# The keep mask of a graph dilation: removals and their transposes summed in PSUM, and the mask written by ScalarE instead of VectorE

## The chip, the cores and the metric

One Trainium2 chip, one of its cores. The metric is the device time of the whole program in microseconds, median over runs. The core has a matrix engine (TensorE, PE in the rows; PEld is its weight load), VectorE (DVE), ScalarE (ACT), GpSimd (POOL) and a queue for transfers (SyncE, SP). Matmuls write into PSUM, which DVE and ACT can read.

## The reference

16 graphs of 1024 nodes with 128 features; `adj` is 16 x 1024 x 1024. Two layers. The first makes three rounds of

```
h = h @ W + b
cos = normalized(h) @ normalized(h).T
h = (adj * cos) @ h            # relu but for the last
```

The second first thins the graph out. Row after row, every `sf`-th neighbour is removed, and each removal also takes the mirrored entry out of the later rows:

```
def step(carry, n):
    row = carry[n]; num = sum(row)
    sf = where(num > 10, (num + 1) // 2, 1)
    rm = row & (cumsum(row) % sf == 0)   # only where mask and num > 1
    carry = carry.at[n].set(row & ~rm)
    carry = carry.at[:, n].set(carry[:, n] & ~rm)
```

It multiplies `adj` by what is left and makes three graph convolutions with batch norms on it. With the inputs given `adj` is symmetric in its pattern, but not in its values.

## The kernel before

The program has a large first part, `layer0`, from 0 to about 1865 us, and then the stages of the second layer. In `layer0` two kinds of work run side by side on the same engines.

The one is the first layer: 48 units (a graph and a round), each of 16 half steps. For a half step PE makes one 128x512 block of the cosine from three fp32r matmuls (L529 to L531), DVE multiplies it by `adj` (L717), and PE aggregates (L538, an fp32 matmul that shows as two rows). The cosine is made two half steps ahead; there are two PSUM tiles for it and three for the product. At fixed half steps of a unit come the short steps of its ends: `ha` the 16 rows of the next projection (L510), `hb` the bias sum on DVE (L695) and then the eight squares with a row sum on ACT (L611), `hc` and `hd` the rest of the row norm, `hf` transposes on PE and a copy on ACT (L622), `evac` the copy of a finished aggregation (L626), and for a new graph `lna` (statistics on DVE, a sqrt on ACT), `lnb` (scaling on DVE, L685), `lnc` (transposes, then relu on ACT) and `posta`/`postb` (transposes, residual sum on DVE).

The other is the thinning, whose result is the mask of entries to keep, stored in DRAM as bytes. It goes in four quads of four graphs. For each of eight blocks of 128 rows a fixpoint of ranks and removals is found (`rule`, `drop`, `again`, L488, L640, L776), then the whole row block is ranked (`wide`: L575 on PE, L650 on ACT, L795 on DVE writes the removals `R`, fp8). After the eight blocks of a quad come its 32 `mask` steps, m = 0 to 127 in all. One makes the mask of 128 rows by 1024 columns in two halves of 512 (j). PE transposes four 128x128 blocks of `R` by a matmul with the identity into half j of the PSUM tile `Dp` (L590). DVE compares: it keeps 1 where the transposed removal is below 0.5 and that is greater than the row's own removal, and writes it into `kp` (L805), one of two tiles. SP stores the tile. PE's matmuls for half j of mask m wait until half j of mask m-1 has been read (semaphore `kp`), and the writing of mask m waits for the store of mask m-2 (semaphores `kps0` and `kps1`).

One plan, made by `layer0_plan` before the program is built, fixes the order on every engine: each engine goes through the same list and does its own part of each step, in that order. Steps of the thinning are spread over the half steps by a weight each; a mask has weight 1, and about one mask step falls to a half step (the 32 of a quad over 34 or 35 half steps). In the mask stretches `hb` occurs at seven places: units 12 and 13, 24 and 25, 35 and 36, and 47. For units 12, 24, 25, 36 and 47 a mask stands in the same half step behind `hb` and another in the next half step; for 13 and 35 the first mask behind `hb` comes in the half step after it.

There is a second writer of masks, `dilate_all`, that runs only where the fixpoint has not settled; it is not touched.

Of the kernel before, what the change touches and what calls it, by code (L numbers as in the profile page):

```python
# [13 lines left out]
ALU = mybir.AluOpType  # L14
ACT = mybir.ActivationFunctionType
# [5 lines left out]
NK = 8  # L21
# [20 lines left out]
def half(j):  # L42
    return slice(j * 512, j * 512 + 512)
# [322 lines left out]
def layer0(nc, A, C, S):  # L366
    with ExitStack() as ctx:
# [3 lines left out]
        T = P.sems("ats0 ats1 at af0 af1 af2 sign low au x ct ru vr sd v8 wd av b1 rw tr kp kps0 kps1")  # L371
# [17 lines left out]
        R = [P.sb(f"R{i}", [128, NK, N], FP8) for i in range(Q)]  # L389
# [12 lines left out]
        kp = [P.sb(f"kp{i}", [128, N], FP8) for i in range(2)]  # L402
        sm = {n: P.sb(f"sm_{n}", [128, Q]) for n in ("t", "sf", "sc", "va", "h", "b", "c", "b2")}
        Dp = P.ps("D", [128, 2, 512])
# [76 lines left out]
        def pe(e):  # L481
            def transposes(src, done):
                for k in range(NK):
                    t = e.transpose(pp[:, k, :], src(k), C["ident"][:])
                t.then_inc(done, 1)

            def count(i, src):
                e.matmul(rank(i)[:, 0:129], src, C["U2"][:, 0:129], start=True, stop=True).then_inc(T["ct"], 1)  # L488

            for kind, *a in plan:  # L490
                if kind == "lnc":
                    g, = a
                    e.wait_ge(E["lnr"], g + 1)
                    if g == 1:
                        e.wait_ge(E["nl"], 1)
                    elif g > 1:
                        e.wait_ge(E["xadd"], g - 1)
                    transposes(lambda k: tmp[:, k, :], E["tln"])
                elif kind == "ha":
                    u, = a  # L500
                    g, i = UNITS[u]
                    if u == 0:
                        e.wait_ge(E["w"], 32)
                    if i == 0:
                        e.wait_ge(E["relu"], g + 1)
                    else:
                        e.wait_ge(E["ev"], 2 * (u - 2) + 2)
                        e.wait_ge(E["nl"], u)
                    for k in range(NK):
                        t = e.matmul(pp[:, k, :], hT[g % 2][:, blk(k)], W[:, i, :], start=True, stop=True)  # L510
                    t.then_inc(E["ph"], 1)
                elif kind == "hf":
                    u, = a
                    e.wait_ge(E["vn"], u + 1)
                    transposes(lambda k: tmp[:, k, :], E["tnh"])
                elif kind == "posta":
                    u, = a
                    e.wait_ge(E["ev"], 2 * u + 2)
                    e.wait_ge(E["nl"], min(u + 2, 3 * G))
                    transposes(lambda k: hT[UNITS[u][0] % 2][:, blk(k)], E["tpost"])  # L520
                elif kind == "cos":
                    idx, = a
                    u, k, j = idx // 16, idx % 16 // 2, idx % 2
                    n, m = nh[u % 2], nl[u % 2]
                    if idx % 16 == 0:
                        e.wait_ge(E["nl"], u + 1)
                    if idx > 1:
                        e.wait_ge(E["ew"], idx - 1)
                    e.matmul(cos[j][:], n[:, blk(k)], n[:, half(j)], start=True, stop=False)  # L529
                    e.matmul(cos[j][:], n[:, blk(k)], m[:, half(j)], start=False, stop=False)  # L530
                    e.matmul(cos[j][:], m[:, blk(k)], n[:, half(j)], start=False, stop=True).then_inc(E["cos"], 1)  # L531
                elif kind == "agg":
                    idx, = a
                    u, k, j = idx // 16, idx % 16 // 2, idx % 2
                    e.wait_ge(E["ew"], idx + 1)
                    if k == 0 and u:
                        e.wait_ge(E["ev"], 2 * (u - 1) + j + 1)
                    e.matmul(acc[j][:], Hr[u % 2][:, k, :], ew[idx % 3][:], start=(k == 0),  # L538
                             stop=(k == NK - 1)).then_inc(E["agg"], 1)
                elif kind == "first":  # L540
                    n, i = a
                    quad, k = divmod(n, NK)
                    if k:
                        e.wait_ge(T["low"], lows(n, i))
                    else:
                        e.wait_ge(T["at"], 64 * quad + 8 * k + 2 * i + 2)
                        if quad and i == 0:
                            e.wait_ge(T["kp"], 64 * quad)
                    others = [q for q in range(NK) if q != k]
                    for q in others:  # L550
                        e.matmul(rank(i)[:, 132:134], AT[i][:, q, blk(k)], (C["two1"] if q < k else C["zero1"])[:],
                                 start=(q == others[0]), stop=(q == others[-1]))
                    count(i, AT[i][:, k, blk(k)])
                elif kind == "again":
                    n, r = a
                    rr = round_of(n, r)
                    for i in range(Q):
                        if i % 2 == 0:
                            e.wait_ge(T["vr"], Q * rr + i + 2)
                        e.wait_ge(T["sd"], Q * rr + i + 1)  # L560
                        count(i, Sd[i][(r + 1) % 2][:])
                elif kind == "wide":
                    n, i, j = a
                    k, K = n % NK, ROUNDS[n % NK]
                    rr = round_of(n, K - 1)
                    if i == 0:
                        e.wait_ge(T["vr"], Q * rr + (2 if j == 0 else 4))
                    elif j == 0:
                        e.wait_ge(T["b1"], Q * n + i)
                    else:  # L570
                        e.wait_ge(T["av"], 8 * n + 2 * i)
                    if j == 0:
                        e.wait_ge(T["sd"], Q * rr + i + 1)
                    for q in range(4 * j, 4 * j + 4):
                        t = e.matmul(Dp[:, j, q * 128 - j * 512:512],  # L575
                                     Sd[i][K % 2][:] if q == k else AT[i][:, q, blk(k)],
                                     C["UL"][:, 0:512 - (q * 128 - j * 512)], start=(q == 4 * j),
                                     stop=(q == 4 * j + 3), skip_group_check=True)
                    t.then_inc(T["wd"], 1)
                elif kind == "mask":  # L580
                    m, = a
                    quad, i, q = m // 32, m % 32 // NK, m % NK
                    for j in range(2):
                        if m % 32 == 0:
                            e.wait_ge(T["rw"], 64 * (quad + 1))
                            e.wait_ge(T["b1"], Q * NK * (quad + 1))
                        else:
                            e.wait_ge(T["kp"], 2 * (m - 1) + j + 1)
                        for b in range(4):
                            t = e.matmul(Dp[:, j, blk(b)], R[i][:, 4 * j + b, blk(q)], C["ident8"][:],  # L590
                                         start=True, stop=True)
                        t.then_inc(T["tr"], 1)

        def act(e):
            for kind, *a in plan:
# [27 lines left out]
                elif kind == "evac":  # L623
                    u, j = a
# [17 lines left out]
                elif kind == "wide":  # L642
                    n, i, j = a
# [9 lines left out]
                    if j == 0:  # L653
                        if n:
                            e.wait_ge(T["av"], 8 * (n - 1) + 2 * i + 2)
                        e.activation(b1[:, i:i + 1], Dp[:, 0, 511:512], ACT.Identity, bias=sm["b"][:, i:i + 1],
                                     scale=sm["sc"][:, i:i + 1]).then_inc(T["b1"], 1)

        def dve(e):
            Dv = Dp[:, :, 0:288].rearrange("p b (i c) -> p b i c", c=144)  # L660
# [2 lines left out]
            for kind, *a in plan:  # L663
# [125 lines left out]
                elif kind == "row_out":  # L789
# [3 lines left out]
                    if quad and k == 0:  # L793
# [1 line left out]
                    e.scalar_tensor_tensor(R[i][:, k, half(j)], v[c % 3][:], sm["sf"][:, i:i + 1],  # L795
                                           Ab[Q * (n % 2) + i][:, half(j)], ALU.not_equal, ALU.is_lt,
                                           saturate=False).then_inc(T["rw"], 1)
                elif kind == "mask":
                    m, = a
                    quad, i, q = m // 32, m % 32 // NK, m % NK  # L800
                    if m > 1:
                        e.wait_ge(T[f"kps{m % 2}"], 16 * (m // 2))
                    for j in range(2):
                        e.wait_ge(T["tr"], 2 * m + j + 1)
                        e.scalar_tensor_tensor(kp[m % 2][:, half(j)], Dp[:, j, :], 0.5, R[i][:, q, half(j)],  # L805
                                               ALU.is_lt, ALU.is_gt, saturate=False).then_inc(T["kp"], 1)

        run(nc, pe, act, dve, pool, sp)

# [901 lines left out]
```

## Time and profile before

| | us |
|---|---|
| median of 3 runs | 3062.6 (3059.87 to 3064.27) |
| the profiled execution | 3064.47 |
| its span in the profile | 3062.4 |
| busy, share of the span: PE | 90% |
| DVE | 77% |
| ACT | 41% |
| POOL | 37% |

Busy is the time in which an engine had at least one instruction in flight. Matmuls overlap one another, so that a matmul's own duration is longer than what it takes of PE; the distance between starts tells the latter. In the order of time, rows of equal instructions in sequence are merged, and "xN" is their number. The bracket behind a row is idle time before it and who ended it.

### The profile page before, as it was taken

How to read it: one execution, taken by the hardware profiler on the slowest of the kernel's cores; microseconds unless marked ns; L12 is line 12 of the kernel's file. 1: busy time of each engine (PE TensorE's matmuls, PEld its weight loads, DVE VectorE, ACT ScalarE, POOL GpSimd, SP SyncE). 2: the span in 40 equal slices, each digit the busy share in tenths (PEclk: the TensorE clock that was granted, in tenths of full speed). 3: DMA queues.
4: the chain of work that ended last, by engine and by line, in shares of the span. 5: the costliest groups of instructions: out<-in, count | busy, mean ns of one | idle time of the engine just before them, and what ended most of it. 6: DMA issues, size and time to landing. Idle time of an engine off the chain costs nothing. (4 is left out here: it accounts for less than half of the span.)

```text
span 3062.4 us, 40924 instructions
## 1 busy us (share of the span) xinstructions
PE 2763.8 (90%) x13317; PEld 1741.2 (57%) x13366; DVE 2352.1 (77%) x6136; ACT 1269.0 (41%) x3748; POOL 1126.7 (37%) x509
## 2 busy tenths in 40 slices
PE   6988999998999998899998995999999979998776
PEld 4655656655656655566655563555555545555666
DVE  4888998898988898888888885756566436775887
ACT  2545541554531555432545420223332234443664
POOL 4434333433432333330000002766666404444772
PEclk9999999999999999999999997999999989998888
DMA  6455346446336336326124014255544229994442
GB/s 217 126 159 179 107 125 198 129 138 198 108 98 209 121 111 207 92 86 201 62 81 154 18 42 171 104 204 218 196 186 184 105 103 394 397 397 171 153 165 117
DMA packets 304077, 492.26 MB, mean 161 GB/s; under 512 B 18544, under 2 KB 196080, under 8 KB 303856
## 3 DMA queue, kind: packets, MB, share of 16 engines
q1 hardware_dynamic: 303856, 489.57, 46.1%
q8 instruction: 108, 1.77, 0.2%
q14 instruction: 113, 0.93, 0.1%
HBM read 422.38 MB, written 67.11 MB: 160 GB/s over the span
## 5 line engine op out<-in xcount | busy, mean ns | idle before, releaser
L478 POOL TENSOR_SCALAR a_AT<-a_ats 128x512 uint8<-128x512 f32 x256 | 503.2, 1970 | 872.3 <-DMA a_ats<-in_adjT 820.4
L538 PE MATMUL a_acc<-a_ew,a_Hr 128*128 128x512 f32 x1536 | 794.0, 599 | 2.6 <-ACT a_hT L626 2.5
L717 DVE TENSOR_TENSOR a_ew<-adj,a_cos 128x512 f32<-128x512 f32 x768 | 522.7, 682 | 141.4 <-PE a_cos L531 140.2
L529 PE MATMUL a_cos<-a_nh 128*128 128x512 f32 x768 | 445.9, 581 | 2.4 <-DVE a_nl L709 2.4
L1286 POOL TENSOR_TENSOR b_dsum<-adj 128x1024 f32<-128x1024 f32 x16 | 141.9, 8868 | 661.1 <-DVE adj L1240 661.1
L538 PEld LDWEIGHTS a_acc<-a_ew,a_Hr 128*128 128x128 f32 x1536 | 291.9, 190 | 72.8 <-issue 2.2
L640 ACT ACTIVATE a_vr<-a_D,a_sm_b,a_sm_sc 128x128 f16<-128x128 f32 x560 | 210.0, 455 | 248.2 <-DVE a_sm_b L766 247.5
L531 PE MATMUL a_cos<-a_nh,a_nl 128*128 128x512 f32 x768 | 306.0, 398 | 0.0
L530 PE MATMUL a_cos<-a_nl,a_nh 128*128 128x512 f32 x768 | 305.9, 398 | 0.0
L1130 PE MATMUL b_acc<-adj,b_h 128*128 128x512 f32 x512 | 224.9, 597 | 23.4 <-DVE adj L1240 23.4
L1290 POOL TENSOR_TENSOR b_dsum<-b_dsum,adj 128x1024 f32<-128x1024 f32 x96 | 225.7, 2351 | 14.1 <-POOL b_dsum L1290 0.5
L1130 PE MATMUL b_acc<-adj,b_z 128*128 128x512 f32 x512 | 223.6, 595 | 0.0
L1387 PE MATMUL c_acc<-adj,c_z 128*128 128x512 f32 x512 | 222.4, 592 | 0.0
L776 DVE SCALAR_TENSOR_TENSOR a_Sd<-a_vr,a_sm_sf,a_X 128x128 fp8e4<-128x128 f16 x560 | 193.9, 371 | 12.1 <-ACT a_vr L640 11.3
L795 DVE SCALAR_TENSOR_TENSOR a_R<-a_v,a_sm_sf,a_Ab 128x512 fp8e4<-128x512 f16 x256 | 186.7, 768 | 9.9 <-ACT a_v L650 9.8
L805 DVE SCALAR_TENSOR_TENSOR a_kp<-a_D,a_R 128x512 fp8e4<-128x512 f32 x256 | 164.6, 685 | 36.9 <-PE a_D L590 30.6
L1477 POOL TENSOR_TENSOR adj<-adj,c_kp 128x1024 f32<-128x1024 f32 x52 | 102.9, 2010 | 242.3 <-DMA adj<-in_adjT 242.3
L611 ACT ACTIVATE a_tmp<-a_Hr 128x128 f32<-128x128 f32 x384 | 113.1, 295 | 187.1 <-DVE a_Hr L695 187.1
L529 PEld LDWEIGHTS a_cos<-a_nh 128*128 128x128 f32 x768 | 147.9, 193 | 63.7 <-issue 55.9
L530 PEld LDWEIGHTS a_cos<-a_nl,a_nh 128*128 128x128 f32 x768 | 148.4, 193 | 57.2 <-issue 56.7
L1130 PEld LDWEIGHTS b_acc<-adj,b_h 128*128 128x128 f32 x512 | 96.9, 192 | 139.7 <-issue 114.2
L531 PEld LDWEIGHTS a_cos<-a_nh,a_nl 128*128 128x128 f32 x768 | 146.1, 190 | 33.7
(198 smaller groups left out, 4875.4 us busy)
## 6 DMA issues: line engine op xcount, KB each, us to landing
adj<-in_adjT SPq DMA_DIRECT2D x108, 1024.0 KB, 12.7
adj<-in_adjT SPq DMA_DIRECT2D x128, 512.0 KB, 5.7
a_ats<-in_adjT SPq DMA_DIRECT2D x256, 256.0 KB, 3.4
a_af<-in_adj SPq DMA_DIRECT2D x256, 256.0 KB, 3.4
scr_keep<-a_kp SPq DMA_DIRECT2D x128, 128.0 KB, 1.8
b_kp<-scr_keep SPq DMA_DIRECT2D x16, 1024.0 KB, 8.4
c_zi<-scr_z SPq DMA_DIRECT2D x32, 512.0 KB, 5.4
c_ai<-scr_ag SPq DMA_DIRECT2D x32, 512.0 KB, 6.4
```

The lines of the kernel that those rows point to most:

```text
L478: e.tensor_scalar(AT[i][:, 4 * h:4 * h + 4, blk(k)].bitcast(U8), ats[h][:], 0.0, ONE8, ALU.is_gt, ALU.mult).then_inc(T["at"], 1)
L529: e.matmul(cos[j][:], n[:, blk(k)], n[:, half(j)], start=True, stop=False)
L530: e.matmul(cos[j][:], n[:, blk(k)], m[:, half(j)], start=False, stop=False)
L531: e.matmul(cos[j][:], m[:, blk(k)], n[:, half(j)], start=False, stop=True).then_inc(E["cos"], 1)
L538: e.matmul(acc[j][:], Hr[u % 2][:, k, :], ew[idx % 3][:], start=(k == 0), stop=(k == NK - 1)).then_inc(E["agg"], 1)
L640: e.activation(vr[:, i, :], rank(i)[:, 0:128], ACT.Abs, bias=sm["b2"][:, i:i + 1], scale=sm["sc"][:, i:i + 1]).then_inc(T["vr"], 1)
L717: e.tensor_tensor(ew[idx % 3][:], adj[g % 2][:, k, half(j)], cos[j][:], ALU.mult).then_inc(E["ew"], 1)
L776: e.scalar_tensor_tensor(Sd[i][(r + 1) % 2][:], vr[:, i, :], sm["sf"][:, i:i + 1], X[i][:], ALU.is_equal, ALU.is_lt, saturate=False).then_ ...
L795: e.scalar_tensor_tensor(R[i][:, k, half(j)], v[c % 3][:], sm["sf"][:, i:i + 1], Ab[Q * (n % 2) + i][:, half(j)], ALU.not_equal, ALU.is_lt ...
L1130: t = e.matmul(acc[j][:], src[:, q, :], adj[n % 3][:, q, half(j)], start=(q == 0), stop=(q == NK - 1))
L1290: e.tensor_tensor(d[:], d[:], b[:, q, :], ALU.add).then_inc(E["ds"], 1)
L1387: t = e.matmul(acc[j][:], z[m % 2][:, q, :], adj[slot(m)][:, q, half(j)], start=(q == 0), stop=(q == NK - 1))
```

## The change

The transposes of the removals are now added to the removals themselves in PSUM: one more matmul for each half, with the identity as weights and the row's own 512 columns of `R` as the moving operand, is issued first and starts the accumulation; the four transposing ones add to it. The sum is 0, 1 or 2. The mask is then relu(1 - sum), written by ACT from that PSUM half into the same fp8 tile. The step `mask` is taken out of DVE's list and put into ACT's at the same place of the plan, with the same waits.

```diff
                         else:
                             e.wait_ge(T["kp"], 2 * (m - 1) + j + 1)
+                        e.matmul(Dp[:, j, :], C["ident8"][:], R[i][:, q, half(j)], start=True, stop=False,
+                                 skip_group_check=True)
                         for b in range(4):
                             t = e.matmul(Dp[:, j, blk(b)], R[i][:, 4 * j + b, blk(q)], C["ident8"][:],
-                                         start=True, stop=True)
+                                         start=False, stop=True, skip_group_check=True)
                         t.then_inc(T["tr"], 1)
```

In `act`:

```diff
+                elif kind == "mask":
+                    m, = a
+                    if m > 1:
+                        e.wait_ge(T[f"kps{m % 2}"], 16 * (m // 2))
+                    for j in range(2):
+                        e.wait_ge(T["tr"], 2 * m + j + 1)
+                        e.activation(kp[m % 2][:, half(j)], Dp[:, j, :], ACT.Relu, bias=1.0, scale=-1.0,
+                                     saturate=False).then_inc(T["kp"], 1)
```

In `dve`:

```diff
-                elif kind == "mask":
-                    m, = a
-                    quad, i, q = m // 32, m % 32 // NK, m % NK
-                    if m > 1:
-                        e.wait_ge(T[f"kps{m % 2}"], 16 * (m // 2))
-                    for j in range(2):
-                        e.wait_ge(T["tr"], 2 * m + j + 1)
-                        e.scalar_tensor_tensor(kp[m % 2][:, half(j)], Dp[:, j, :], 0.5, R[i][:, q, half(j)],
-                                               ALU.is_lt, ALU.is_gt, saturate=False).then_inc(T["kp"], 1)
```

## Rows read from the trace of the kernel before

**Rows 1.** The page, first part: busy us, share of the span, instructions.
```profile
PE 2763.8 (90%) x13317; PEld 1741.2 (57%) x13366; DVE 2352.1 (77%) x6136; ACT 1269.0 (41%) x3748; POOL 1126.7 (37%) x509
```

**Rows 2.** Busy us of each engine in the four mask stretches, granted clock, DMA.
```profile
core 0: us, PE busy (x) PEld busy (x) DVE busy (x) ACT busy (x) POOL busy (x), PEclk, DMA share, GB/s
439.80:530.70 90.90, 83.67 (x504) 55.41 (x504) 77.96 (x159) 13.60 (x46) 27.79 (x15) 0.96 0.64 203
890.00:980.00 90.00, 82.28 (x494) 53.82 (x493) 77.68 (x160) 12.61 (x45) 25.06 (x13) 0.98 0.66 209
1340.00:1430.00 90.00, 83.61 (x504) 55.25 (x502) 79.48 (x163) 12.90 (x46) 11.53 (x6) 0.98 0.51 162
1786.80:1862.20 75.40, 74.22 (x457) 48.20 (x457) 65.67 (x105) 6.70 (x24) 0.00 (x0) 1.00 0.22 76
```

**Rows 3.** Groups by line: busy us, mean ns | idle just before, who ended it.
```profile
L590 PE MATMUL a_D<-ident,a_R 128*128 128x128 fp8e4 x1024 | 84.9, 221 | 23.8 <-DVE a_kp L805 22.0 <-DVE a_R L795 0.8
...
L805 DVE SCALAR_TENSOR_TENSOR a_kp<-a_D,a_R 128x512 fp8e4<-128x512 f32 x256 | 164.6, 685 | 36.9 <-PE a_D L590 30.6
```

**Rows 4.** Order of time (start, us) in the first stretch: layer norm, mask, PE's wait.
```profile
450.15 2.14 DVE L685 TENSOR_SCALAR a_tmp<-a_tmp,a_lnmv,a_lnrs 128x128 f32<-128x128 f32 x8
...
452.20 1.29 DVE L805 SCALAR_TENSOR_TENSOR a_kp<-a_D,a_R 128x512 fp8e4<-128x512 f32 x2
...
452.95 0.40 PE L590 MATMUL a_D<-ident,a_R 128*128 128x128 fp8e4 x4 [2.18 <-DVE a_kp L805]
```

**Rows 5.** PE in order of time, fourth stretch: a step without a mask, one with.
```profile
1792.21 1.02 PE L538 MATMUL a_acc<-a_ew,a_Hr 128*128 128x512 f32 x2
...
1793.77 1.02 PE L538 MATMUL a_acc<-a_ew,a_Hr 128*128 128x512 f32 x2
...
1795.82 1.02 PE L538 MATMUL a_acc<-a_ew,a_Hr 128*128 128x512 f32 x2
1796.68 0.61 PE L590 MATMUL a_D<-ident,a_R 128*128 128x128 fp8e4 x8
...
1797.41 0.40 PE L530 MATMUL a_cos<-a_nl,a_nh 128*128 128x512 f32 x1
1797.64 0.40 PE L531 MATMUL a_cos<-a_nh,a_nl 128*128 128x512 f32 x1
1797.88 1.02 PE L538 MATMUL a_acc<-a_ew,a_Hr 128*128 128x512 f32 x2
```

**Rows 6.** PE's groups by shape: matmuls with fp8 weights, 512 and 128 columns.
```profile
L575 PE MATMUL a_D<-UL,a_AT 128*128 128x512 bf16 x180 | 68.8, 382 | 8.7 <-ACT a_b L656 7.3 <-ACT a_v L650 1.4
...
L575 PE MATMUL a_D<-UL,a_AT 128*128 128x128 bf16 x224 | 49.1, 219 | 0.0
```

**Rows 7.** ACT's groups by shape, to 1865 us.
```profile
L634 ACT ACTIVATE a_Ab<-a_af 128x512 fp8e4<-128x512 f32 x256 | 153.6, 630 | 26.4 <-DMA a_af<-in_adj 26.2
L611 ACT ACTIVATE a_tmp<-a_Hr 128x128 f32<-128x128 f32 x384 | 113.1, 295 | 187.1 <-DVE a_Hr L695 187.1
L650 ACT ACTIVATE a_v<-a_D,a_b,a_sm_sc 128x512 f16<-128x512 f32 x128 | 99.5, 777 | 17.9 <-DVE a_R L795 3.7 <-PE a_D L575 0.8
...
L626 ACT ACTIVATE a_hT<-a_acc 128x512 f32<-128x512 f32 x96 | 57.6, 600 | 153.6 <-PE a_acc L538 153.5
L622 ACT ACTIVATE a_nh<-a_pp 128x1024 fp32r<-128x1024 f32 x48 | 49.4, 1028 | 135.8 <-PE a_pp L484 135.8
```

**Rows 8.** Order of time in the fourth stretch, around the one `hb`.
```profile
1805.84 1.02 PE L538 MATMUL a_acc<-a_ew,a_Hr 128*128 128x512 f32 x2
...
1806.34 0.68 DVE L717 TENSOR_TENSOR a_ew<-adj,a_cos 128x512 f32<-128x512 f32 x1
...
1806.93 1.22 DVE L695 TENSOR_TENSOR a_Hr<-a_pp,a_rows 128x1024 f32<-128x1024 f32 x1
```

**Rows 9.** Who waited for whom: us in total, times, longest us.
```profile
DVE a_kp L805 <- DMA scr_keep<-a_kp: 6.1, 6, 1.4
```

## The prediction

> **What bounds the kernel now.** I read the page's first part, then the four stretches in which the keep masks are made, then who waits for whom in them, and last the order of time in single steps. TensorE (PE) is busy for 90% of the span, VectorE (DVE) for 77% and ScalarE (ACT) for 41% [rows 1]. By these shares the change moves work from the second busiest engine to an idle one, and adds some to the busiest. What that is worth is read only where the masks are made, in four stretches of about 32 masks each, 346.3 us together [rows 2]. There ACT is nearly idle (12.6 to 13.6 us of 90, and 6.7 of 75.4), while PE and DVE both run near full: 83.67 and 77.96 of 90.90 in the first, 74.22 and 65.67 of 75.40 in the fourth. So the two share the limit. In the fourth PE is it, with 1.2 us left over. In the first three PE lacks 7.2, 7.7 and 6.4 us (length less busy), and its clock, which is granted at one of two levels (2.4 and 1.2 GHz), has means of 0.96, 0.98 and 0.98 of the higher.
>
> The same idle time by its cause: over all 1024 transposing matmuls PE stood 22.0 us waiting for DVE's mask (L805) [rows 3]. Where it comes from is seen at 450 us: DVE has the residual sum and the layer-norm scaling to do (L685, 2.14 us), writes the mask after it (452.20), and PE, which needs the mask tile's PSUM half read, idles 2.18 us [rows 4]. Between such places PE has no gap. From one aggregation (L538) to the next it takes 1793.77-1792.21 = 1.56 us without a mask step and 1797.88-1795.82 = 2.06 us with one [rows 5], so the eight 128-column matmuls of a mask cost PE 0.50 us, 62 ns each. The 221 ns of their row [rows 3] is their length from start to end, much of it overlapped, and no price. DVE in such a step does two masks of 0.685 us and one product L717 of 0.68 us, 2.05 us of work beside PE's 2.06.
>
> **What is removed from DVE.** 256 instructions at 685 ns (counted in halves of a mask), 175 us [rows 3] (the page's 164.6 us counts overlapped starts once). Of it only what PE now waits for can come back: the 22.0 us of waits, and the clock that fell behind them. Over the first three stretches that is 90.9 x 0.04 + 90 x 0.02 + 90 x 0.02 = 7.2 us [rows 2]. With DVE at 0.68 us per step against PE's 2 us and more, even the 3.6 us that it spends at a time on the residual sum and layer norm is made good before the next product is due. I take back all of it: -29.2 us. Outside the four stretches no mask is made and nothing changes.
>
> **What is added to PE.** One pass of 512 fp8 columns for each half, 256 in all. No such row exists. From below: a wide matmul of L575 with fp8 weights takes 219 ns at 128 columns and 382 at 512 [rows 6], 163 ns for 384 more columns, so 0.217 us for 512. From above: the 512-column fp32r passes of the cosine start 1797.64-1797.41 = 0.23 us and 1797.88-1797.64 = 0.24 us apart, weights loaded under the one before [rows 5]. I take 0.22: 256 x 0.22 = 56.3 us (0.217 gives 55.6, 0.235 gives 60.2). The furthest bound below is the 62 ns of one small mask matmul, 16 us. The added weight load is counted in the spacing, as those of L530 and L531 are. None of it is hidden: PE has no gap left once the masks come in time. Accumulating instead of overwriting is taken at nothing, since the cosine's three passes accumulate at that same spacing.
>
> The Trainium skill ("TensorE: Matmul & The Clock Gate", Back-to-back issue gap) puts a sustained stream of weight load and matmul at about 131 ns for 512 columns, and the isolated gap at N/2.4 + 2.5 ns, 216 ns. The trace contradicts the first (0.23 us in a stream with loads, rows 5) and supports the second. By 131 ns the pass would cost an estimated 33.5 us in place of 56.3, and the forecast would be 23 us lower.
>
> **What is added to ACT.** 256 instructions, 128x512 fp8 out of PSUM. The nearest rows: 600 ns for the copy L626 from PSUM with constants, 630 for the fp8 sign L634, 777 for L650 with both scale and bias from memory [rows 7]. So an operand from memory adds about 90 ns. If the constant bias of one is read as a column, 0.69 us is the value, and I take it; the ends are 0.60 and 0.78. Sum 177 us of work, in steps that now last 2.06 + 0.44 = 2.5 us, where a mask takes ACT 1.38 us. It fits, and costs nothing by itself.
>
> But ACT works in the order of the plan, and PE's next mask half waits for the one before to be read. What ACT has queued ahead of a mask now counts. Evacuations (0.60 us) and copies of 1024 columns (1.03 us) end before PE has done its mask, cosine and aggregation (2.5 us). The sqrt of the layer norm waits for 2.3 us of statistics on DVE; counted from the end of the cosine it is ready near 3.6 us, its mask half at 4.2, and PE comes for it at 4.4 after an aggregation, a mask, another product and the transposes. That just fits. The squares of the row norm (`hb`) do not. They wait for DVE's bias sum L695, which waits its turn behind L717. After the cosine's end (PE's aggregation starts at 1805.84 [rows 8]): product from 0.2 to 0.88 us, bias sum of 1.22 to 2.1 (1806.93 to 1808.15 now, because the masks are ahead of it), ACT's squares 8 x 0.295 = 2.36 us [rows 7] to 4.55, mask halves at 5.2 and 5.9. PE arrives for the first at 0.86 + 0.94 + 1.56 = 3.4 us. It waits 1.9 us and some 0.2 more for the second half: 2.1 us. In the plan `hb` falls into the mask stretches seven times; five times with a mask in its own step and in the next, 5 x 2.1 = 10.5 us, twice with the masks one step later, 2 x 0.4 = 0.8. Sum 11.3 us. Waits of this length are of the size after which the clock fell before (2.18 us at 452.95, clock 0.96 in that stretch). I take two falls at 1.8 us each, what the second and the third stretch lost with 0.98: +3.6 us.
>
> **Moved with it.** The wait for the store of the mask two before moves from DVE to ACT: 6.1 us in 6 waits, the longest 1.4 [rows 9]. SP's order is the same, its store is issued when the mask is written, and PE sees the wait only through ACT; behind it on ACT stand the same masks as before. Nothing more.
>
> **The sum.** -22.0 - 7.2 + 56.3 + 11.3 + 3.6 = +42.0 us. The profiled execution took 3064.47 us (span 3062.4), 1.9 above the median of 3062.6, so on the median 3104.6, in round numbers 3105.
>
> **The rivals.**
> R1, ACT holds PE more often. The sqrt of the layer norm just fits; if the mask takes 0.78 us or the handshakes are slower, its seven places and others give waits of 1 to 2 us, another 11 us, with 4 us of clock and the pass at 0.235: +42.0 + 11 + 4 + 3.9 = +60.9, about 3124. For it: three engines in turn. Against it: ACT's 1.1 us of slack in each step.
> R2, the squares do not hold PE. If the product and the bias sum come early enough, or the semaphores allow a step of run-ahead that I missed, the 14.9 us go: +27.1, 3090. Against it: the two PSUM halves are the only ones.
> R3, the other side: faster. The new pass costs PE no more than the small matmuls around it, 62 ns, since the price is that of issuing one and not of its columns. Then 256 x 0.0625 = 16.0 us against 29.2 back, and with ACT never late it is -13.2: 3049. It decides below 29.2/256 = 0.114 us per pass. Against it stands the 163 ns between 128 and 512 columns [rows 6].
> R4, PE is not full. PE's weight loads are busy for 48.20 of 75.40 us in the fullest stretch [rows 2]; if matmul busy overstates it, part of the new passes lies in room that the rows don't show. Half of them hidden: +13.6, 3076. Against it: the unbroken spacing of rows 5, where no start is free. The Trainium skill ("Perfetto Trace Analysis", Identifying the Most-Contended Engine) says that matmul occupancy is no good measure and weight-load busy is; by it the 64% here means headroom, against which the start-to-start times speak.
>
> **How the numbers follow.** Forecast (+33 to +52) 0.62; R1 0.15; R2 0.12; R4 and a cheap pass 0.06, of which 0.03 end within 0.2%; R3 0.05. The change is certain to do its work on ACT instead of DVE; no case for that. Within 0.2% means 6 us, about what a measurement of this kernel can tell from none. Faster 0.05, same 0.03, slower 0.92. The range leaves out R3, R4 and the far end of R1: 3086 to 3125.
>
> **What would show it.** The fourth stretch near 91 us in place of 75.4 (32 x 0.44 = 14 us for the passes, 2 us for its one `hb`, less a little waiting); the first three 94 to 101 us each, the passes being partly paid by what PE waited. PE's step with a mask 2.50 us. DVE's busy share down by 165 us, ACT's up by 150 to 180. PE's waits for a mask on ACT near 11 us, in places of about 2 us after L611. The fourth stretch under 83 us would make the price of the pass wrong; the first three shorter than before would bring R3; waits for ACT over 20 us, R1.

## The result, and the profile after

The changed kernel takes 3086.23 us (median of 4 runs, 3085.45 to 3088.13) against 3061.23 us (3059.15 to 3064.27): ratio 1.0085, 95% interval 1.0072 to 1.0097. Run again beside the experiments it gave 3084.93 us and 1.0080 (1.0066 to 1.0094). It is slower by 25 us. I had forecast slower by 42, 3105 us, with a range of 3086 to 3125: the side is right and the size is off by 17 us. The value lies 0.2 us above the lower end of the range, and the second measurement 1 us below it.

The first part of the page after (busy us, share, instructions):

```profile
PE 2809.2 (91%) x13622; PEld 1767.0 (57%) x13622; DVE 2194.5 (71%) x5880; ACT 1403.9 (46%) x4004; POOL 1126.9 (37%) x509
```

Against [rows 1] DVE has lost 157.6 us of work and ACT gained 134.9, and PE has gained 45.4 us. DVE's work did not set the time: PE's busy time grew by 45.4 us, its idle time shrank by 24.1, and the span grew by the difference, 21.3 us (3083.7 - 3062.4). The masks' lines, by shape (busy us, mean ns | idle before, who ended it):

```profile
L589 PE MATMUL a_D<-a_R,ident 128*128 128x512 fp8e4 x256 | 97.1, 379 | 8.5 <-ACT a_kp L666 7.7 <-DVE a_R L805 0.8
...
L592 PE MATMUL a_D<-ident,a_R 128*128 128x128 fp8e4 x1024 | 98.9, 219 | 0.0
```

PE waits for the mask 7.7 us where it waited 22.0 [rows 3]. The four stretches, each now cut from the start of its first mask matmul to the start of its last one (length, busy us by engine, granted clock):

```profile
440.50:533.80 93.30, 91.77 (x570) 60.33 (x569) 41.90 (x97) 46.04 (x109) 28.88 (x15) 1.00 0.61 199
890.50:985.40 94.90, 91.82 (x572) 60.32 (x571) 43.79 (x99) 45.22 (x107) 25.00 (x13) 1.00 0.64 202
1344.20:1437.50 93.30, 91.76 (x572) 60.42 (x570) 41.91 (x97) 44.60 (x106) 11.53 (x6) 1.00 0.51 160
1794.20:1881.30 87.10, 85.52 (x518) 54.35 (x519) 28.10 (x40) 39.88 (x86) 0.00 (x0) 1.00 0.19 64
```

Cut in the same way, the stretches of the kernel before are:

```profile
440.00:530.80 90.80, 83.57 (x506) 55.37 (x505) 77.86 (x159) 13.60 (x46) 27.89 (x15) 0.96 0.64 203
892.50:983.30 90.80, 82.51 (x507) 54.27 (x505) 78.44 (x160) 12.40 (x44) 25.06 (x13) 0.98 0.66 209
1343.20:1431.20 88.00, 81.61 (x506) 54.54 (x505) 77.44 (x159) 11.53 (x44) 11.53 (x6) 0.98 0.53 169
1786.90:1861.00 74.10, 73.07 (x454) 47.88 (x455) 64.44 (x103) 6.53 (x23) 0.00 (x0) 1.00 0.22 75
```

The sums are 368.6 and 343.7 us: 24.9 us arise here, where the spans differ by 21.3, so the rest of the program is 3.6 us shorter. I take that remainder for scatter: no instruction in the rest was changed, and over the ten profiled executions of this document it took between 2709 and 2719 us. In the fourth stretch, where PE waited least before, the change costs most: 13.0 us, against 2.5, 4.1 and 5.3 in the others.

In single steps, PE in the fourth stretch (start, us):

```profile
1809.87 1.02 PE L538 MATMUL a_acc<-a_ew,a_Hr 128*128 128x512 f32 x2
1810.73 0.38 PE L589 MATMUL a_D<-a_R,ident 128*128 128x512 fp8e4 x1
1810.95 0.39 PE L592 MATMUL a_D<-ident,a_R 128*128 128x128 fp8e4 x4
1811.17 0.38 PE L589 MATMUL a_D<-a_R,ident 128*128 128x512 fp8e4 x1
1811.38 0.39 PE L592 MATMUL a_D<-ident,a_R 128*128 128x128 fp8e4 x4
...
1812.35 1.02 PE L538 MATMUL a_acc<-a_ew,a_Hr 128*128 128x512 f32 x2
```

From aggregation to aggregation it takes 2.48 us in place of 2.06 [rows 5]. That is 0.42 us for two passes, 0.21 each, and 128 x 0.42 = 53.8 us in all.

And the place behind the squares, the one in the fourth stretch, first PE and then ACT:

```profile
1816.62 1.02 PE L538 MATMUL a_acc<-a_ew,a_Hr 128*128 128x512 f32 x2
...
1819.10 1.02 PE L538 MATMUL a_acc<-a_ew,a_Hr 128*128 128x512 f32 x2
1821.65 0.39 PE L589 MATMUL a_D<-a_R,ident 128*128 128x512 fp8e4 x1 [1.54 <-ACT a_kp L666]
...
1823.34 1.02 PE L538 MATMUL a_acc<-a_ew,a_Hr 128*128 128x512 f32 x2
```

```profile
1818.67 0.31 ACT L613 ACTIVATE a_tmp<-a_Hr 128x128 f32<-128x128 f32 x1 [1.90 <-DVE a_Hr L705]
...
1821.03 1.05 ACT L666 ACTIVATE a_kp<-a_D 128x512 fp8e4<-128x512 f32 x2
```

ACT gets the bias sum, makes the squares from 1818.67 on, and writes the waiting mask only at 1821.03. PE's step from 1819.10 to 1823.34 is 4.24 us instead of 2.48, so 1.76 us are lost. The plan has five such places in the mask stretches, and the trace has exactly five waits of PE for ACT's mask.

### The profile page after: what moved, and what is told of

Read it like the earlier page. It is cut to its first block and busy times, and to the rows that moved or that the text cites. A ratio compares the mean times of both kernels' runs of the same rounds, so it can differ in the third digit from the quotient of the medians.

```text
span 3083.7 us, 41485 instructions
## 1 busy us (share of the span) xinstructions
PE 2809.2 (91%) x13622; PEld 1767.0 (57%) x13622; DVE 2194.5 (71%) x5880; ACT 1403.9 (46%) x4004; POOL 1126.9 (37%) x509
## 5 line engine op out<-in xcount | busy, mean ns | idle before, releaser
L786 DVE SCALAR_TENSOR_TENSOR a_Sd<-a_vr,a_sm_sf,a_X 128x128 fp8e4<-128x128 f16 x560 | 191.4, 369 | 12.7 <-ACT a_vr L642 11.7
L666 ACT ACTIVATE a_kp<-a_D 128x512 fp8e4<-128x512 f32 x256 | 138.6, 593 | 120.6 <-PE a_D L592 114.1
L575 PE MATMUL a_D<-UL,a_AT 128*128 128x384 bf16 (+3 forms) x896 | 156.4, 299 | 13.7 <-ACT a_b L658 7.3
```

The source lines that it names most:

```text
L786: e.scalar_tensor_tensor(Sd[i][(r + 1) % 2][:], vr[:, i, :], sm["sf"][:, i:i + 1], X[i][:], ALU.is_equal, ALU.is_lt, saturate=False).then_ ...
```

## The experiments

All ratios are to the kernel before on the same chip (3062.10 us for e1 to e4, 3060.88 for e5 to e7 and the changed kernel run again; the first two lines of the table are the first pair). "Stretches" is the sum of the four lengths, cut as above. "Waits" is PE's idle time before a mask matmul by the trace, in us. "Floor" is what PE needs in the stretches without a wait: 359.5 us with the passes (shown under `e4_mask_before_squares`), 359.5 - 53.8 = 305.7 us without.

| kernel | us | ratio (95%) | stretches | PE's waits for a mask |
|---|---|---|---|---|
| before | 3061.23 | | 343.7 | 22.0 |
| changed | 3086.23 | 1.0085 (1.0072 to 1.0097) | 368.6 | 7.7 |
| e1_no_pass | 3042.21 | 0.9929 (0.9907 to 0.9951) | 323.6 | 10.3 |
| e2_pass_on_dve | 3088.79 | 1.0083 (1.0062 to 1.0104) | 372.2 | 10.5 |
| e3_two_passes | 3137.92 | 1.0240 (1.0216 to 1.0263) | 421.2 | 5.5 |
| e4_mask_before_squares | 3077.69 | 1.0043 (1.0027 to 1.0060) | 359.5 | 0 |
| e5_split_ln | 3044.17 | 0.9949 (0.9935 to 0.9962) | 328.0 | 8.6 |
| e6_split_wide | 3044.62 | 0.9950 (0.9936 to 0.9963) | 325.4 | 0.2 |
| e7_split_narrow | 3044.15 | 0.9951 (0.9935 to 0.9966) | 325.8 | 7.9 |

**e1_no_pass**: ScalarE writes the mask, without the added matmul.

```diff
-                        e.matmul(Dp[:, j, :], C["ident8"][:], R[i][:, q, half(j)], start=True, stop=False,
-                                 skip_group_check=True)
...
-                                         start=False, stop=True, skip_group_check=True)
+                                         start=True, stop=True)
```

> The changed kernel without the added pass: the four transposing matmuls overwrite as before, and ScalarE writes relu(1 - transposes). It leaves out the row's own removals from the mask. Theory A (the pass costs PE 0.21 us each of 256, all of it on the path; the masks on ScalarE give back the waits for VectorE, which are worth more than the 22.0 us counted because each wait also loses the overlap of the matmul before it, about 0.17 us in 39 places, and with 8 us of clock come to some 37 us): 54 us below the changed kernel less 2 to 3 us of longer waits behind the squares, about 3035 us, and 26 us below the kernel before. Theory B (the waits gave back only the 29 us of the forecast and the pass is cheaper than its spacing, 0.18 us or less, because part of it lies in gaps): about 3042 us or more. R3 or R4 of the prediction (pass nearly free): above 3060.

Measured: 3042 us, the value that B named, not A's 3035. The total alone would have decided for the wrong theory. In the trace the price of the pass is A's; what is larger than expected are the waits behind the squares, since PE now comes earlier (fourth stretch, PE):

```profile
1785.33 1.02 PE L538 MATMUL a_acc<-a_ew,a_Hr 128*128 128x512 f32 x2
1788.31 0.88 PE L590 MATMUL a_D<-ident,a_R 128*128 128x128 fp8e4 x8 [1.96 <-ACT a_kp L664]
...
1789.77 1.02 PE L538 MATMUL a_acc<-a_ew,a_Hr 128*128 128x512 f32 x2
1790.63 0.61 PE L590 MATMUL a_D<-ident,a_R 128*128 128x128 fp8e4 x8
...
1791.83 1.02 PE L538 MATMUL a_acc<-a_ew,a_Hr 128*128 128x512 f32 x2
```

The step takes 4.44 us against 2.06, so 2.38 us are lost. Four of the five waits are of this size and one is of 1.66 us; five times 2.38 would be 11.9 us. The clock fell in two of the stretches (means 0.98 over 84.7 and 83.0 us, 3.4 us). 323.6 - 305.7 = 17.9 us is these two and 2.6 more, of which 1.2 stand in two steps with further waits of 0.40 us; for the rest I have no cause. So without the pass the change would have been a gain of 20 us (3062.10 - 3042.21), and the pass takes all of it and more.

**e2_pass_on_dve**: the kernel before with the pass.

```diff
+                        e.matmul(Dp[:, j, :], C["ident8"][:], R[i][:, q, half(j)], start=True, stop=False,
+                                 skip_group_check=True)
...
-                                         start=True, stop=True)
+                                         start=False, stop=True, skip_group_check=True)
```

> The kernel before with the added pass, VectorE still writing the mask in its old instruction (the sum below 0.5 and greater than the row's own removal is the same mask). Theory A: PE's step with a mask becomes 2.48 us, VectorE's 1.97 us then fits with 0.5 us to spare, so part of the 37 us of waits and clock goes even without ScalarE: 54 us for the passes less some 15 to 20, 3095 to 3100 us, 10 to 15 us above the changed kernel. Theory B: 46 us or less for the passes with the waits unchanged, at most 3107, or near 3090 with the same waits shrinking.

Measured: 3089 us, below what A expected and at the second of B's numbers (the waits shrink), though the price of the pass is A's. By its ratio it can't be told apart from the changed kernel. PE's groups:

```profile
L592 PE MATMUL a_D<-ident,a_R 128*128 128x128 fp8e4 x1024 | 98.9, 219 | 0.0
L589 PE MATMUL a_D<-a_R,ident 128*128 128x512 fp8e4 x256 | 97.1, 379 | 11.3 <-DVE a_kp L807 10.5 <-DVE a_R L797 0.8
```

The waits for DVE halve without taking anything from DVE: its 1.97 us per step are hidden under a step that the pass has made 2.48 us long. Over the floor of 359.5 stand 12.7 us, where the kernel before has 343.7 - 305.7 = 38.0. So of the 38.0 us that the change "gives back", 25 would also have come from its own longer step alone. Once the pass is there, ScalarE as the writer is worth 12.7 us and costs 368.6 - 359.5 = 9.1 us behind the squares: 3.6 us net. The two halves of the change do not add up: over its floor each kernel has 38.0 us (neither), 17.9 (ScalarE alone, e1), 12.7 (the pass alone, e2) and 9.1 (both).

**e3_two_passes**: the pass made twice.

```diff
+                        e.matmul(Dp[:, j, :], C["ident8"][:], R[i][:, q, half(j)], start=False, stop=False,
+                                 skip_group_check=True)
```

> The changed kernel with the added pass made twice (the sum is then up to 3 and relu(1 - sum) is the same mask). ScalarE has time enough, PE has none left. Theory A: 256 x 0.213 = 54 us more, less 5 x 0.4 us because PE comes later to the masks behind the squares: 3138 us. Theory B: under 46 us more, below 3132 us.

Measured: 3137.92 us, 3138 expected. The matmul that follows `layer0` (the sum of the flags) starts at 1942.5 us, against 1889.0 in the changed kernel: 53.5 us more for 256 passes. The stretches alone are 52.6 us longer, while PE's waits behind the squares shrink by 2.2 us (7.7 to 5.5), so that the passes themselves take some 55 us, 0.21 each. The steps show the passes 0.21 to 0.22 us apart (PE):

```profile
1882.20 0.38 PE L589 MATMUL a_D<-a_R,ident 128*128 128x512 fp8e4 x1
1882.41 0.38 PE L591 MATMUL a_D<-a_R,ident 128*128 128x512 fp8e4 x1
1882.63 0.39 PE L594 MATMUL a_D<-ident,a_R 128*128 128x128 fp8e4 x4
```

**e4_mask_before_squares**: the changed kernel, on ScalarE the mask of the same half step goes ahead of the squares.

```diff
-            for kind, *a in plan:
+            order = list(plan)
+            for p, s in enumerate(plan):
+                if s[0] == "hb":
+                    q = next(i for i in range(p + 1, len(plan)) if plan[i][0] in ("cos", "agg", "mask"))
+                    if plan[q][0] == "mask":
+                        order[p:q + 1] = plan[p + 1:q + 1] + [s]
+            for kind, *a in order:
```

> The changed kernel with ScalarE's order changed at the five places where the squares of the row norm stand directly before a mask in one half step: the mask is written first, then the squares. Theory A (ScalarE's squares hold up the mask and so PE by 1.76 us at each of the five, 8.8 us): the mask of the next half step is late by 0.3 to 0.5 us instead, so 6 us below the changed kernel, near 3080 us, and PE's waits for ScalarE fall from 7.7 us to under 2. Rival (the squares are not what PE waits for, as R2 has it, or the row norm's own chain then becomes late): no change, 3086 us, or slower.

Measured: 3077.69 us, and the stretches are 9.1 us shorter than in the changed kernel, all five waits gone without the remnant I had allowed for. PE has no idle time (length and PE's busy time are the same number, the first two values of each row):

```profile
439.10:530.60 91.50, 91.50 (x572) 60.42 (x570) 42.38 (x97) 45.97 (x109) 29.05 (x15) 1.00 0.63 203
889.30:980.50 91.20, 91.20 (x570) 60.35 (x569) 43.63 (x99) 44.91 (x107) 24.98 (x13) 1.00 0.65 210
1340.00:1431.50 91.50, 91.50 (x571) 60.47 (x570) 41.57 (x97) 44.34 (x106) 11.53 (x6) 1.00 0.53 164
1787.20:1872.50 85.30, 85.30 (x519) 54.43 (x520) 28.01 (x40) 39.80 (x86) 0.00 (x0) 1.00 0.20 65
```

This is the floor: everything left is PE's own work, and the kernel is still slower than before. R2 falls: the squares did hold PE.

**e5_split_ln, e7_split_narrow, e6_split_wide**: masks shared out by step; those on VectorE go without the pass. One semaphore for each writer, counted when the program is built; `acts` holds the numbers of ScalarE's masks. The three differ only in `acts`: 15, 12 and 47 masks. (The last two lines of the cut stand in ScalarE's and in VectorE's list.)

```diff
+                            kept(e, m - 1, j + 1)
+                        if m in acts:
+                            e.matmul(Dp[:, j, :], C["ident8"][:], R[i][:, q, half(j)], start=True, stop=False,
+                                     skip_group_check=True)
...
+                                         start=m not in acts, stop=True, skip_group_check=True)
...
+                elif kind == "mask" and a[0] in acts:
...
+                elif kind == "mask" and a[0] not in acts:
```

> The masks are shared out by step: VectorE writes them as before, without the added pass, but the 15 masks that fall into the first half step of a new graph's layer norm or two and three after it are ScalarE's, with the pass (two semaphores, one for each writer). The four mask stretches have a floor of 305.7 us of PE's own work (359.5 us without a wait, less 128 x 0.42). Theory A (what ScalarE gives back is nearly all at the layer norm, VectorE fits elsewhere): 305.7 + 15 x 0.42 = 312 us and about 9 us of waits of VectorE that stay at the row norms, 321 us in place of 343.7: some 20 us below the kernel before, 3040 us. Rival (VectorE lacks time everywhere in the stretches, so its waits only move to the next step): 335 us or more, 3053 us.

> As the split by the layer norm, with 12 masks on ScalarE (only those two and three half steps into it, so VectorE's statistics are followed by its own mask). Theory A: one wait of about 1 us more at each of six statistics against 3 x 0.42 us saved, 325 us in the stretches, 3044 us. Rival (VectorE lacks time everywhere): slower than that by several us.

> As the split by the layer norm, but ScalarE also takes the masks one and four half steps into it and those of the half steps of the row norm's bias sum, scaling and last subtraction (47 masks; behind the bias sum the mask stands before the squares). Theory A: no waits, 305.7 + 47 x 0.42 = 325.5 us in the stretches, 3044 us, some 4 us above the narrower split. Rival (VectorE lacks time everywhere): this one is the faster of the two.

Measured: 3044 us for all three, 16 to 17 us below the kernel before and 41 below the changed one. Their times can't be told apart. The stretches of the wide split came out at 325.4 us, 325.5 expected, and PE is busy for all but 0.3 us of them (the first two):

```profile
439.00:522.60 83.60, 83.60 (x534) 56.94 (x533) 62.58 (x131) 28.46 (x74) 28.91 (x15) 1.00 0.69 221
883.90:968.40 84.50, 84.50 (x540) 57.31 (x538) 60.87 (x129) 29.32 (x76) 25.51 (x13) 1.00 0.69 226
```

The narrow split came out as expected too (325.8 us, 325 expected). The split by the layer norm missed: 328.0 us, 321 expected. Its waits by their cause:

```profile
L615 PE MATMUL a_D<-ident,a_R 128*128 128x128 fp8e4 x1024 | 85.5, 219 | 9.9 <-DVE a_kp L844 8.2 <-DVE a_R L834 0.8 <-ACT a_kp L695 0.4
```

These are 8.6 us in 28 waits, but the stretches are 328.0 - (305.7 + 15 x 0.42) = 16.0 us over their floor. Each wait costs 0.26 us more than its row says (in the narrow split 15.1 us over the floor with 7.9 us in 29 waits, 0.25). It is seen in single steps of the kernel before, behind those of [rows 8]:

```profile
1807.90 1.02 PE L538 MATMUL a_acc<-a_ew,a_Hr 128*128 128x512 f32 x2
...
1809.41 0.40 PE L590 MATMUL a_D<-ident,a_R 128*128 128x128 fp8e4 x4 [0.20 <-DVE a_kp L805]
...
1810.39 1.02 PE L538 MATMUL a_acc<-a_ew,a_Hr 128*128 128x512 f32 x2
```

From aggregation to aggregation this step takes 2.49 us, 0.43 over the 2.06, where the trace gives 0.20 us idle. Steps laid beside the same steps of e4, less 0.21 us for each pass, say the same: an idle row of 0.20 us goes with 0.42 us of length in eight steps of the kernel before, one of 1.54 with 1.75 in the changed kernel, one of 2.02 with 2.35 in e2. My reading of it: an idle row begins at the modelled end of the matmul before it, and a matmul of 219 ns that takes 56 ns of PE's time ends 0.16 us after the next one could have started. The 0.16 covers most of the difference; what the rest is remains open.

**after_again**

> The changed kernel itself, beside the others on one chip, to have its distance from the kernel before and from the kernel with the mask before the squares. All theories: 25 us above before, 9 us above that kernel by its stretches (368.6 against 359.5 us).

Measured: 1.0080, 24 us over before, 25 expected; its stretches are 368.4 us, 8.9 more than those of e4. Its whole time lies 7.2 us above e4's, but that one ran on another chip.

## Why the prediction was right, and where it was off

The mechanism was the forecast one: PE bounds the stretches once the masks come in time, the pass is paid in full, and what comes back is less. The size was not. The sum was +42.0 and is +24.9 in the stretches (21.3 to 25 in all), below the forecast's own +33 to +52. The range held the value only because it also took in R2 (+27.1, 3090 us), in which the squares do not hold PE, and e4 shows that they do. That the measured time fell inside, by 0.2 us, was luck. By its terms:

1. **The pass**: 56.3 forecast, 53.8 measured. The step gives 0.21 for a pass, at the lower row that I had (0.217), not 0.22; e3 confirms it with some 55 us for 256 more.
2. **What comes back**, "I take back all of it: -29.2 us". All of it did come back, but it was 38.0 (343.7 - 305.7). This is the term that was mis-sized, by 8.8 us. I took the waits at the 22.0 us of the idle rows. The kernel before has 39 of these waits (total us, times, longest):

```profile
PE a_D L590 <- DVE a_kp L805: 22.0, 39, 2.8
```

   With 0.25 us more for each, as e5 and e7 have it, that is 9.8 us beside the 22.0. The clock's part is about the 7.2 of the forecast: it was granted at half for 13.6 us of the four stretches together, which is worth 6.8, and in the changed kernel never. Together 39.0 for 38.0. So I read the idle rows as the whole price of a wait, and they are not.
3. **The squares**: 11.3 forecast, 9.1 measured (e4 takes exactly this away). Five waits, at the places named. They cost 1.76 us each, not 2.1. Counted from PE's aggregation at 1816.62, ACT ends the squares after 4.41 us (4.55 forecast) and PE goes on after 5.03 (5.2), so the first wait is near the forecast one; the 0.2 us more for the second half did not come, for the two halves take ACT 1.05 us together and not 1.38. ACT's mask half took 0.59 us, not 0.69: the constant bias costs nothing. The two places with a mask one step later, taken at 0.8, cost nothing.
4. **The clock after the new waits**: 3.6 forecast, 0 measured. In all four stretches the granted clock is 1.00. What makes it fall these runs don't settle, for the length of the wait alone does not tell: before, it fell behind four of six waits of 2.2 to 2.8 us; in e1 behind one of 1.66 and one of four of 1.96; in e2 behind none, with 1.86, 2.00 and 2.02 among them.

53.8 - 38.0 + 9.1 = 24.9. The errors are all on one side, and that of the returned waits is half of the 17 us. Two slips beside them changed nothing: half of the passes hidden would be +13.9 in R4, not +13.6, and the 62 ns of a small mask matmul is the difference of two steps divided by eight, where their starts are 56 ns apart.

R1 fell: the sqrt of the layer norm was to "just fit", and the trace has no wait for ACT's mask there. R2 fell by e4. R3 and R4 fell by e3: no part of a pass is hidden. The Trainium skill ("Perfetto Trace Analysis", Identifying the Most-Contended Engine) judges TensorE's headroom by its useful work against the peak and by the busy share of weight loads, not by that of matmuls. By the second of these the 64% of the fourth stretch meant headroom to R4, and the runs speak against it: in the changed kernel weight loads are busy for 62% of that stretch (54.35 of 87.10), and e3 pays each further pass in full. The 131 ns that the Trainium skill ("TensorE: Matmul & The Clock Gate", Back-to-back issue gap) gives for a matmul of 512 columns in a stream with weight loads isn't seen either: it is 0.21 us in e3, in such a stream.

Of the signs that I had named, the fourth stretch came out at 87.1 us (near 91 forecast) and PE's step at 2.48 (2.50); the first three were 93.3, 94.9 and 93.3, about the lower end of 94 to 101, since more came back there than I had taken. ACT gained 134.9 us, not 150 to 180, with 0.59 us for a half and overlapped starts counted once.

One thing I didn't see: I credited ScalarE with the whole return. e2 shows that two thirds of it come with the longer step alone.

## What to carry to other kernels

Here two engines shared the bound step by step. Relieving one by adding a little to the other paid only in the steps in which the first was late: 12 to 47 masks of 128 were enough for 17 us gained, where all 128 lost 25. Price what is added to the bound engine by start-to-start times for every instance, and what is given back only where a wait stands, with the step as long as it will be after the change: a longer step hid 25 of the 38 us by itself. An idle row of PE understated a wait by about 0.25 us here; take the step's length with and without it.

## What was not expected of the hardware

A relu with a scale and a bias of constants takes 0.593 us for 128x512 out of PSUM into fp8, the same as the copy L626 (0.600), while L650 with both from memory takes 0.777. The Trainium skill ("ScalarE: Activation LUTs", What ACT_TABLE_LOAD costs) gives about 93 ns for each operand from memory and none for constants; the trace agrees: 0.777 - 0.593 is twice 0.092, though the two rows also differ in what they write (f16 and fp8).

```profile
L666 ACT ACTIVATE a_kp<-a_D 128x512 fp8e4<-128x512 f32 x256 | 138.6, 593 | 120.6 <-PE a_D L592 114.1
```

The small matmuls with fp8 data start 56 ns apart, with a weight load for each. Eight in a row take 0.61 us [rows 5], that is seven distances and the last one's own 219 ns; behind a 512-column pass four of them take 0.22 us (1811.17 - 1810.95).
